# Graph network, count stage: stripes of edges gathered from their first edge on in three tiles of 128 instead of four aligned ones

## The reference

```
dst = sorted node of each edge, src = node at its other end
L0: e = leaky(s_src[src] + s_dst[dst]); att = softmax of e over the edges of one src
    x = x + elu(segment_sum(att * h[dst], src))
L1: three times: x = layernorm(relu(segment_sum(norm * (x @ W)[src], dst) + b)) + x
L2: five times: m = h @ W[l]; agg = segment_sum(m[src], dst); h = GRU(agg, h); then two dense layers
L3: agg = segment_sum(edge_weight * x[src], dst)
    x = x + leaky((agg + x) @ W1.T + b1 + (agg * x) @ W2.T + b2)
```

## Time and profile before

| what | value |
|---|---|
| median of 3 runs | 2469.88 us (2468.3 to 2472.03) |
| the profiled execution's own time | 2460.7 us |
| its span, first to last instruction | 2458.9 us |
| TensorE busy | 2203.4 us (90% of the span) |
| VectorE busy | 1088.8 us (44%) |
| ScalarE busy | 769.0 us (31%) |
| GpSimd busy | 629.5 us (26%) |
| prepare, up to the first operation of counts | 0 to 101.2 us |
| counts, up to VectorE's last window | 101.2 to 357.8 us |
| zero fills (WT<-zero, line 671), page's list of DMA issues | 39 of 980 KB, 5.1 us each from issue to landing |
| last operations of counts and visits | 357.8 to 371.0 us |

### The profile page before, as it was taken

How to read it: one execution, slowest core, us unless ns; L and a number is a source line. 1 busy time by engine, 2 the same in 40 slices (tenths; PEclk the granted TensorE clock), 3 DMA queues, 4 the chain that set the end, 5 groups by cost and what they waited for, 6 DMA issues and landing times.

```text
span 2458.9 us, 28185 instructions
## 1 busy us (share of the span) xinstructions
PE 2203.4 (90%) x10179; PEld 1230.9 (50%) x10180; DVE 1088.8 (44%) x3043; ACT 769.0 (31%) x1405; POOL 629.5 (26%) x425
## 2 busy tenths in 40 slices
PE   4677768889868999598999999999999999998998
PEld 3444438755544555244445554455445554454444
DVE  7499988999973456433121121222112211112202
ACT  3455547788852333222111111111111111112200
POOL 1000004300003434143444434443444344410000
PEclk9899995699998999799999999999999999999999
DMA  5444431111212111323222232223222322124583
GB/s 165 149 171 159 169 124 2 27 53 52 74 58 34 1 27 22 93 52 81 43 46 31 46 76 26 38 40 71 46 30 45 67 37 34 22 57 160 212 304 102
DMA packets 178582, 187.22 MB, mean 76 GB/s; under 512 B 101916, under 2 KB 165582, under 8 KB 174379
## 3 DMA queue, kind: packets, MB, share of 16 engines
q1 hardware_dynamic: 108474, 134.73, 16.6%
q0 software_dynamic: 56720, 1.28, 6.8%
q10 hardware_dynamic: 13260, 49.53, 5.6%
HBM read 100.83 MB, written 84.66 MB: 75 GB/s over the span
## 4 chain that ended last, share of the span: by engine, by line
PE 53%; DMA 3%; DVE 1%; issue 1%; ACT 0%; DVEq 0%; ACTq 0%
PE banks L1607 24%; PE banks L1632 21%; PE banks L1729 5%; DMA feat<-hnD 3%; PE banks L1685 1%; PE banks L1593 1%; PE banks L1694 0%; PE banks L1747 0%; DMA out_dram<-big 0%; DVE HN L1900 0%; DVE banks L1895 0%; ACT banks L1792 0%; DVE HN L1897 0%; PE banks L1744 0%; PE banks L1710 0%
## 5 line engine op out<-in xcount | busy, mean ns | idle before, releaser
L808 POOL DMA_INDIRECT WT<-lists x391 | 615.5, 1574 | 861.8 <-DMA WT<-lists 846.9
L1607 PE MATMUL banks<-big,feat 125*128 125x500 f16 (+1 forms) x3150 | 606.8, 353 | 19.4 <-DMA feat<-hnD 15.2
L1607 PEld LDWEIGHTS banks<-big,feat 125*128 125x128 f16 x3150 | 306.5, 97 | 309.9 <-DMA feat<-hnD 16.0
L1632 PE MATMUL banks<-H,U 128*128 128x500 f32 (+1 forms) x756 | 302.8, 541 | 9.4 <-issue 9.3
L1632 PE MATMUL banks<-aT,V 128*128 128x500 f32 (+1 forms) x756 | 296.4, 538 | 3.0 <-DVE HN L1900 3.0
L771 PE MATMUL banks<-ohp,ohs 128*125 128x500 f16 x628 | 164.4, 384 | 66.9 <-DVE ohp L689 66.9
L1632 PEld LDWEIGHTS banks<-aT,V 128*128 128x128 f32 x756 | 143.1, 190 | 145.1 <-issue 97.4
L1888 DVE SCALAR_TENSOR_TENSOR HN<-banks,bh,HN 128x500 f32<-128x500 f32 (+1 forms) x70 | 47.8, 682 | 378.5 <-ACT HN L1790 354.4
L1632 PEld LDWEIGHTS banks<-H,U 128*128 128x128 f32 x756 | 142.6, 191 | 139.2 <-issue 101.6
L689 DVE TENSOR_SCALAR ohp<-pairs,wcol 128x500 f16<-128x500 f16 x628 | 177.3, 351 | 0.0
L1790 ACT ACTIVATE HN<-banks,bs 128x500 f32<-128x500 f32 (+1 forms) x70 | 44.3, 633 | 381.5 <-PE banks L1632 381.5
(11 more groups left out here) (273 smaller groups left out, 2269.4 us busy)
## 6 DMA issues: line engine op xcount, KB each, us to landing
big<-WT ACTq DMA_DIRECT2D x25, 1562.5 KB, 7.5
WT<-zero SPq DMA_DIRECT2D x39, 980.0 KB, 5.1
hTD<-HN SPq DMA_DIRECT2D x40, 250.0 KB, 2.1
hnD<-stg SPq DMA_DIRECT2D x32, 250.0 KB
feat<-hnD SPq DMA_DIRECT2D x4, 2000.0 KB
H<-hTD SPq DMA_DIRECT2D x16, 500.0 KB, 4.9
work<-xhD SPq DMA_DIRECT2D x28, 250.0 KB
WT<-lists POOLq DMA_INDIRECT x391, 3.0
```

Source lines behind the costliest of these rows:

```text
L808: nc.gpsimd.indirect_dma_start(out=WT, out_offset=bass.IndirectOffsetOnAxis(ap=lists[:, 0, t - first:t - first + 1], axis=0), in_=lists[:, ...
L1607: last = nc.tensor.matmul(SUMS[s % 2][half][:, 0:wid(ch)], rows_, A[:, j, cols(ch)], start=(j == 0 and part == 0), stop=(j == T - 1 and pa ...
L1632: last = nc.tensor.matmul(PS[bank][:, 0:w], wt_[:, kt, g:g + 128], v[:, kt, 0:w], start=(n == 0), stop=(n == len(terms) - 1))
```

## The change

Stripes are now gathered from their first edge on. Edges are stored in DRAM as one number each, dst*3125 + src (nearD), and can be gathered from any edge on. Since a stripe then need not start at a tile's boundary, SPAN is 3 tiles of 128 edges. To find the first and last edge of each stripe, four first gathers bring the tile in which the stripe begins and the one in which it ends (two halves of up to 128 stripes each, WH = 2), VectorE looks for edges inside the stripe (inside, ends), and writes the edge numbers for six more gathers (tilei). Edges of a neighbouring stripe that a tile also holds fall outside the 500 pairs of the window and match nothing.

The gathered numbers are parted into comb and sib by VectorE after the gather (gk, gs), where csD held both before. Padding and foreign edges stay harmless because sib and nodes are now counted from 1. The table of visits is now computed per stripe on partitions (cover), and brought to one row by six small TensorE products with ident (rep, row_t) and three copies from PSUM (row_c); the last of them is needed by the visits, in which edges already covered are masked out (place, past, left). The zero tile is half as wide (245 numbers) and each fill uses it eight times instead of four; the bytes are the same.

```diff
-SB = -(-NW * 4 // LANE)
+WH = -(-NW // LANE)
...
-SPAN = 4
+SPAN = 3
+SB = SPAN * WH
...
-ZN = 490
-ZW = 4 * ZN
+ZN = 245
+ZW = 8 * ZN
...
-    csD = dram("csD", (EG * LANE, 2 * LANE))
+    nearD = dram("nearD", (EG * LANE * LANE, 1))
...
+        near1 = sb("near1", [128, EG, LANE])
+        rows4 = near
+        lanes = sb("lanes", [128, 4, LANE])
...
-        EDGES, CS, ABC, CAND, ROWS, LESS, SCALED, DIGITS = range(1, 9)
-        MADE = 15
+        EDGES, CS, ABC, CAND, TILES_, ROWS, REP, LESS, SCALED, DIGITS = range(1, 11)
+        MADE, ALL = 7, 18
...
+                iota(low[:], [[LANE, WH]], 0, 1)
+                iota(lanes[:, 0:2], [[0, 2], [1, LANE]], -LANE, 0)
+                iota(lanes[:, 2:4], [[0, 2], [1, LANE]], 1, 0)
+                iota(step[:], [[LANE, SPAN], [0, WH]], 0, 0)
                 iota(pairs[:], [[1, WC]], 0, 0)
-                iota(nodes[:], [[1, P]], 0, 0)
+                iota(nodes[:], [[1, P]], 1, 0)
+                iota(place[:], [[LANE, EG * LANE]], 0, 1)
...
+                pool.wait_ge(dve_did, TILES_)
+                pool.wait_ge(cs_out, 16)
+                for b in range(4):
+                    nc.gpsimd.indirect_dma_start(out=edge4[:, b, :], out_offset=None, in_=nearD.rearrange("(t e) o -> t (e o)", e=LANE),
+                                                 in_offset=bass.IndirectOffsetOnAxis(ap=tli[:, b:b + 1], axis=0)).then_inc(found, 16)
                 pool.wait_ge(dve_did, ROWS)
-                pool.wait_ge(cs_out, 16)
-                for b in range(SB):
-                    nc.gpsimd.indirect_dma_start(out=gath[:, b].rearrange("p a e -> p (a e)"), out_offset=None, in_=csD,
-                                                 in_offset=bass.IndirectOffsetOnAxis(ap=tilei[:, b:b + 1], axis=0)).then_inc(gathered, 16)
+                for k in range(SPAN):
+                    for hf in range(WH):
+                        nc.gpsimd.indirect_dma_start(out=gath[:, 0, k, hf, :], out_offset=None, in_=nearD,
+                                                     in_offset=bass.IndirectOffsetOnAxis(ap=tilei[:, k, hf:hf + 1], axis=0)).then_inc(gathered, 16)
+                pool.wait_ge(found, 64)
                 pool.wait_ge(gathered, 16 * SB)
...
-                sp.wait_ge(dve_did, CS)
-                sp.dma_start(csD.rearrange("(g t) e -> t g e", g=EG), cs[:].rearrange("t g a e -> t g (a e)")).then_inc(cs_out, 16)
+                sp.wait_ge(dve_did, EDGES)
+                sp.dma_start(nearD.rearrange("(g t e) o -> t g (e o)", g=EG, t=LANE), near1[:]).then_inc(cs_out, 16)
...
+                pe.wait_ge(dve_did, REP)
+                pe.wait_ge(u_c, 1)
+                for q in range(3):
+                    for hf in range(WH):
+                        a = (q % 2 * WH + hf) * LANE
+                        last = nc.tensor.matmul(PS[6 + q // 2][:, a:a + LANE], rep[:, q, hf, :], ident[:], start=True, stop=True)
+                last.then_inc(row_t, 1)
                 pe.wait_ge(dve_did, LESS)
-                pe.wait_ge(u_c, 1)
-                for b in range(SB):
+                pe.wait_ge(row_c, 1)
+                for b in range(SPAN):
                     if b >= 2:
                         pe.wait_ge(gath_c, b - 1)
                     for q in range(2):
-                        last = nc.tensor.transpose(PS[6 + b % 2][:, q * 128:(q + 1) * 128], gath[:, b, q], ident[:])
+                        for hf in range(WH):
+                            a = (q * WH + hf) * LANE
+                            last = nc.tensor.transpose(PS[6 + b % 2][:, a:a + LANE], gath[:, q, b, hf, :], ident[:])
                     last.then_inc(gath_t, 1)
                 for i in range(10, LATE):
                     folded(i)
-                pe.wait_ge(gath_c, SB)
+                pe.wait_ge(gath_c, SPAN)
...
+                    nc.scalar.copy(wcol[:, :, b * WH * LANE:(b + 1) * WH * LANE],
+                                   PS[6 + b % 2][:].rearrange("p (a r) -> p a r", a=2)).then_inc(gath_c, 1)
...
+                V_.scalar_tensor_tensor(near1[:], ef[:, 1], float(N), ef[:, 0], ALU.mult, ALU.add).then_inc(dve_did, 1)
+                V_.scalar_tensor_tensor(key[:], ef[:, 0], float(N), ef[:, 1], ALU.mult, ALU.add)
 
                 done(V_.tensor_scalar(part[:], ef[:, 0], -float(P // 2), 1.0 / P, ALU.add, ALU.mult))
                 done(V_.tensor_scalar(part[:], part[:], ROUND, None, ALU.add))
                 done(V_.tensor_scalar(part[:], part[:], -ROUND, None, ALU.add))
                 V_.scalar_tensor_tensor(cs[:, :, 0, :], ef[:, 1], float(T), part[:], ALU.mult, ALU.add)
-                V_.scalar_tensor_tensor(cs[:, :, 1, :], part[:], -float(P), ef[:, 0], ALU.mult, ALU.add).then_inc(dve_did, 1)
+                done(V_.scalar_tensor_tensor(cs[:, :, 1, :], part[:], -float(P), ef[:, 0], ALU.mult, ALU.add))
+                V_.tensor_scalar(cs[:, :, 1, :], cs[:, :, 1, :], 1.0, None, ALU.add).then_inc(dve_did, 1)
...
-                done(V_.memset(start[:], 0.0))
-                done(V_.tensor_scalar(start[:, 0:NW], red[:, 0, :], -1.0, FAR, ALU.mult, ALU.add))
-                done(V_.tensor_scalar(start[:, 0:NW], start[:, 0:NW], float(ET - 1), None, ALU.min))
-
-                done(V_.tensor_scalar(hit[:], near4[:], 0.0, None, ALU.is_ge))
-                done(V_.scalar_tensor_tensor(hit[:], near4[:], 3.0, hit[:], ALU.is_le, ALU.mult))
-                done(V_.tensor_tensor(near4[:], near4[:], hit[:], ALU.mult))
-                done(V_.tensor_reduce(place[:], near4[:], X, ALU.add))
-                done(V_.tensor_tensor(picked[:], start[:].rearrange("p (b j) -> p b j", j=32),
-                                      hit[:, None, :].to_broadcast([128, SB, 32]), ALU.mult))
-                done(V_.tensor_reduce(tile[:], picked[:], X, ALU.add))
-                done(V_.tensor_scalar(tile[:], tile[:], place[:], None, ALU.add))
-                V_.tensor_copy(tilei[:], tile[:]).then_inc(dve_did, 1)
-
-                done(V_.tensor_scalar(place[:], place[:], -float(WC // 4), None, ALU.mult))
-                done(V_.tensor_scalar(woff[:], woff[:], place[:], None, ALU.add))
-
-                done(V_.tensor_scalar(vis[:, 0, :], start[0:1, 0:NW], float(SPAN), None, ALU.add))
-                done(V_.tensor_tensor(vis[:, 1, :], red[0:1, 1, :], vis[:, 0, :], ALU.subtract))
+                flat = rows4[:].rearrange("p a e -> p (a e)")
+                done(V_.memset(rows4[:], 0.0))
+                done(V_.tensor_scalar(flat[:, 0:NW], red[:, 0, :], -1.0, FAR, ALU.mult, ALU.add))
+                done(V_.tensor_scalar(flat[:, 0:NW], flat[:, 0:NW], float(ET - 1), None, ALU.min))
+                done(V_.tensor_scalar(flat[:, 2 * LANE:2 * LANE + NW], red[:, 1, :], -1.0, 0.0, ALU.add, ALU.max))
+
+                done(V_.tensor_tensor(rows4[:], rows4[:], ident[:, None, :].to_broadcast([128, 4, LANE]), ALU.mult))
+                done(V_.tensor_reduce(tl[:], rows4[:], X, ALU.add))
+                V_.tensor_copy(tli[:], tl[:]).then_inc(dve_did, 1)
+                done(V_.tensor_scalar(tl[:], tl[:], float(LANE), None, ALU.mult))
+                spread(5, 15)
+
+                dve.wait_ge(made, ALL)
+                done(V_.tensor_scalar(low[:], low[:], float(WIN * N), -1.0, ALU.mult, ALU.add))
+                dve.wait_ge(found, 64)
+                done(V_.tensor_tensor(edge4[:].rearrange("p (a h) e -> p a h e", a=2), edge4[:].rearrange("p (a h) e -> p a h e", a=2),
+                                      low[:, None, :, None].to_broadcast([128, 2, WH, LANE]), ALU.subtract))
+                done(V_.tensor_scalar(inside[:], edge4[:], 1.0, None, ALU.is_ge))
+                done(V_.scalar_tensor_tensor(inside[:], edge4[:], float(WIN * N), inside[:], ALU.is_le, ALU.mult))
+                done(V_.tensor_tensor(inside[:], inside[:], lanes[:], ALU.mult))
+                V_.tensor_reduce(ends[:, 0:2], inside[:, 0:2], X, ALU.min)
+                done(V_.tensor_reduce(ends[:, 2:4], inside[:, 2:4], X, ALU.max))
+                done(V_.tensor_tensor(ends[:], ends[:], tl[:], ALU.add))
+                done(V_.tensor_scalar(e0[:], ends[:, 0:2], float(LANE), None, ALU.add))
+                V_.tensor_tensor(tilei[:], e0[:, None, :].to_broadcast([128, SPAN, WH]), step[:], ALU.add).then_inc(dve_did, 1)
+
+                done(V_.tensor_scalar(cover[:, 2], e0[:], float(SPAN * LANE), None, ALU.add))
+                V_.tensor_scalar(two[:, 0], cover[:, 2], -(LANE - 1) / 2.0, 1.0 / LANE, ALU.add, ALU.mult)
+                done(V_.tensor_scalar(two[:, 1], ends[:, 2:4], (LANE - 1) / 2.0, 1.0 / LANE, ALU.add, ALU.mult))
+                done(V_.tensor_scalar(two[:], two[:], ROUND, None, ALU.add))
+                done(V_.tensor_scalar(two[:], two[:], -ROUND, None, ALU.add))
+                V_.tensor_copy(cover[:, 0], two[:, 0])
+                done(V_.tensor_tensor(cover[:, 1], ends[:, 2:4], cover[:, 2], ALU.is_gt))
+                done(V_.tensor_tensor(two[:, 1], two[:, 1], two[:, 0], ALU.subtract))
```

(69 more changed lines are left out.)

26 lines of the change are left out of this document (11 added, 15 removed).

## The result

| | before | after |
|---|---|---|
| median (range), us | 2469.71 (2468.3 to 2472.03) | 2491.32 (2481.82 to 2499.64) |
| profiled execution, us | 2460.7 | 2481.82 |
| count stage begins, us from the span's start | 101.3 | 126.2 |
| count stage, us | 256.6 | 247.5 |
| TensorE's granted clock in it | 0.99 | 0.70 |

After takes 1.0085 times as long, 95% interval 1.0048 to 1.0123; 2439 (2418 to 2457) was predicted. Between the two profiled spans lie +21.1 us: +24.9 ahead of the counts, -9.0 in them (unrounded) instead of the -51.1 predicted, +0.8 in the visits, and +4.4 in the stages behind, which the diff does not touch.

The account below looks back on a forecast made before the run. TensorE's chain of waits, in stages untouched, bounds the page; VectorE's pace bounds the counts, digD's landing the preparation. Counts -51.1, preparation +19.4, visits +1.0 give -30.7 us: 2469.88 to 2439 us, range 2418 to 2457.

Parts of the forecast that it names:

- The transfers of the counts: Count stage: whether half-sized fill pieces delay the dig loads; taken to cost nothing, otherwise 23 us.
- I take zero: Count stage: 980-byte fill pieces cost nothing, since bytes seem to set a fill's time and not pieces.
- the 2.6 and the 5.2 that stood as bounds: Count stage, fill burst: 2.6 us if only bytes count, 5.2 if every piece costs the same whatever its length.
- makes dig loads late: +23: Rival for the count stage: half-sized fill pieces make dig loads late, +23 us on the forecast, 2462; 9%.
- the lower clock in the preparation alone (2.0 us): Preparation: TensorE resumes from idleness at 1.2 GHz, costing up to 2.5 us more; 2.0 taken.
- The counts' pace: Count stage: three tiles instead of four bring it from 256.6 to 205.5 us, windows 1.30 apart, gain 51.1 us.
- merge chain: Count stage: product, eq, merge and gap take S+2.81, later than VectorE's 2.46; three windows take 3.91 us instead of 3.69.
- wrong if: Signs against the forecast: windows at 1.23 us, TensorE waiting for dig loads, or digD issued before 90.
- first rival: Count stage runs at VectorE's pace: -63 + 20.4 gives 2427 us; 15%.
- The preparation: Before the counts: VectorE waits for rep's product, digits follow, TensorE stands for a trow copy; stage ends 19.4 us later.
- The visits: Two visits, each with a one-column operation, a wait and two register addresses more, 0.5 us each: +1.0 us.

Follow-up runs that it names:

- e8: The kernel before with fills in 980-byte pieces (zero tile of 245 numbers), nothing else changed: 2468.43 us, ratio 1.0006 to before.
- e11: The changed kernel with fills in 1024-byte pieces instead of 980: 2427.98 us, ratio 0.9859 to the kernel before.
- e1: The changed kernel with its fills in pieces of 1960 bytes again: 2435.93 us, ratio 0.9889 to the kernel before.
- e4: The changed kernel, narrow fills kept, plus one unused 480-column product per window in the first 152 windows: 2459.11 us, ratio 0.9964 to before.
- e6: The kernel before making one-hots of three of four tiles, but with four products (the first done twice): 2427.28 us, ratio 0.9844 to before.
- e5: The kernel before making and multiplying only three of four tiles, fourth tile's edges left out, wide fills: 2413.23 us, ratio 0.9779 to before.
- e9: e1 with the preparation reordered (SCALED before the row_t wait, two trow copies amid the digits, rep's product earlier): 2418.93 us, ratio 0.9797 to before.
- e3: The changed kernel, narrow fills kept, with each merge one window later: 2444.5 us, ratio 0.9909 to the kernel before.
- e12: e9 (wide fills, reordered preparation) with each merge one window later: 2410.88 us, ratio 0.9782 to the kernel before.
- e13: The changed kernel, narrow fills kept, with only the preparation reordered as in e9: median 2462.67 us, ratio 0.9996 to the kernel before.
- e10: The kernel before with fills in 1024-byte pieces (zero tile of 256 numbers): one run of 2463.13 us.

## Why the prediction was wrong

**The step that failed** stands in "The transfers of the counts": "I take zero". The fill moved 980 KB in 2.6 us, and the prediction took from this that bytes set its time and not pieces; that row had pieces of 1960 bytes and could not say it of 980. They take 4.3 us per fill (e8), between the 2.6 and the 5.2 that stood as bounds. The Trainium skill, "DMA: Bandwidth & Descriptors", Specifications, has transfers at line rate from 512 bytes on; e8 shows 980-byte pieces at about 205 GB/s for most of a burst and e11 1024-byte ones at 345, so here the measurement goes against the page.

**The second term at nothing is the clock.** The rival's "makes dig loads late: +23" is about what the waits add up to, 21.2 us in 24 gaps. It left out what TensorE's clock does after a stall. The clock is at its lower level for 147 us of the stage (126 to 167, 208 to 218, 242 to 283, 297 to 310, 331 to 372), and a window takes 1.75 to 1.80 us there instead of 1.245: 147 x (1 - 1.245 / 1.80) = 45, or 42 with 1.75, of the 52 us by which the stage is longer than e1's. The rest, 7 to 10, goes with the late loads at full clock, near the 10.7 between e4 and e6. Of the 45 us, 12 belong to the first 41 us of the stage, ahead of the first late load; e5 and e9 have such an entry with wide fills, so it cannot be laid on the pieces. The other 33 come behind late loads. That a fall costs so much is shown by e3 and e4: with the stalls left in, the stage is 36 and 24 us shorter when other gaps in TensorE's queue are closed or filled. The prediction counted the lower clock in the preparation alone (2.0 us), and took 2.4 GHz for every window of the counts.

Why three products and not four is shown only in outline: with four, the clock comes back within 7 us in every profile. With three, the waits of the merges for eq are 41 us of the stage, the same in after, e1 and e5. They are harmless at full clock, where VectorE is the limit (e1 has them and a stage of 195.5, e12 has none and 197.0). At the lower level TensorE's queue is the limit and they lie in it; without them e3's falls are short. The Trainium skill, "TensorE: Matmul & The Clock Gate", Part 1, lets the gate follow how busy the engine has been recently. That agrees with e4; it fits less easily that after's row from 242 to 282 shows 40.00 busy us of 40 at 0.50. Such a row hides short stops: the waits of 242 to 282 have 14 of its weight loads standing 5.7 us for eq. Which stops count was not found.

**The counts' pace.** The merge chain was mis-sized. With the fills mended (e1) windows stand at 1.245 us, not 1.30: 195.5 us against 205.5, VectorE's pace, the "wrong if" of the prediction and its first rival. The timeline of e1 shows a merge's weights starting 0.05 us after eq's end (0.13 was taken from the rows of before), and gaps following a merge by 0.18 instead of 0.38:

```profile
181.84 0.60 ACT L800 ACTIVATE eq<-banks 128x512 bf16<-128x512 f32 x1
...
182.49 0.17 PEld L825 LDWEIGHTS banks<-wp,eq 128*128 128x128 bf16 x4 [0.50 <-ACT eq L800]
```

Both margins, read at the old pace, held slack that nobody needed to use. The sum missed by 10 us in the other direction: had the fills cost nothing, the span would have been 2426.6 us (e1's profile) against 2428.2 predicted, and the time 0.9889 x 2469.7 = 2442 against 2439. That near hit is partly luck: in e1's profile 10 us too much here, 4 too little in the preparation (start 124.7 for 120.5) and 5 behind the counts.

**The preparation** went by the predicted mechanism: VectorE waiting for rep's product, the digits behind it, TensorE standing for the trow copy. +24.9 instead of +19.4. DIGITS fell near 93 instead of 88.1, digD's issue at 100.58 instead of 95.2: 5.4 us, of which TensorE's later arrival at rep's product (60.0 instead of 55.0) is 5, which the prediction had taken as fixed: the folded jobs start 1.0 us later, TensorE waits 3.31 us for ScalarE ahead of the last of them instead of 1.01, and these take 7.12 us instead of 5.43, with the clock at 0.50 from 54.5 to 57.9. e9 and e13 show that the order causes most of the 24.9: 15.4 and 18.6 us of the start come back. The other 6 to 10 were not traced.

**The visits**: 4.92 us apart instead of 4.57, +0.8 against +1.0. Right.

**Open.** The untouched stages behind the counts are 4.4 us longer, and likewise in every kernel with three tiles: from the counts' end to the span's end 2101.0 us before, 2106.3 after, 2106.4 in e1, 2106.7 in e5 and up to 2109.5 in e13, against 2103.0 and 2101.0 in e8 and e10, which have four. In e5 the visits' code is that of before, so the edit of the visits is not the cause; none was found. The spread of after's runs (18 us against 4) goes with the clock as far as the whole-run figures tell (0.918 in the fastest run, 0.908 in the slowest); when and for how long it falls was read in single profiles only.

## What to carry to other kernels

A transfer that is hidden at the old pace has to be priced at the new one, with its own piece length: narrow pieces cost nothing in the kernel before and some 50 us in the changed one. When an edit takes work off TensorE, ask what its granted clock will be afterwards, above all behind the first late load or a hole; look for the short waits in its queue (here a merge that could come one window later) before trusting a row that says it is busy. And a duration read from a queue with slack is an upper bound, not a term.

## What was unexpected of the hardware

- 980-byte pieces from SBUF to HBM: a 980 KB fill occupies the engines for 4.3 us, at about 205 GB/s in most of it; 1024-byte pieces run at 345, 1960-byte ones need 2.6 us.
- More work made a kernel faster: 152 idle products brought the ratio from 1.0085 to 0.9964, while the clock in the stage went from 0.70 to 0.98 and the waits for digits stayed (21.2 and 23.6 us).
- After one idle stretch the clock stayed at 1.2 GHz for the first 41 us of the stage in e5, with TensorE busy 37.63 of 39.30 us; with the same three products it was back after 5 us in e11 and 6 in e1.
